# Pipelined attention with score runs of eight heads, a maximum and an exponent over two PSUM banks, and another order of products within a step

## The chip, the cores and the metric

The kernel runs on one core of one Trainium2 chip. The metric is the device time of one execution in microseconds (us); lower is better. The engines are TensorE (PE in the rows; PEld are its weight loads), VectorE (DVE), ScalarE (ACT), GpSimd (POOL) and SyncE (SP), which issues most transfers.

## What is computed

Two decoder layers on x, 32 batches of 128 tokens of width 128, in fp32: self-attention, cross-attention and a mixture of experts, then an attention with shared heads, a masked cross-attention and a second mixture. The change concerns the three attentions with 16 heads of width 8. For one of them the reference has

```python
Q, K, V = proj(q, w_q, b_q), proj(k, w_k, b_k), proj(v, w_v, b_v)   # per head: 128 x 8
scores = jnp.einsum('bhsd,bhtd->bhst', Q, K) / sqrt(8)
attn = jax.nn.softmax(scores, axis=-1)       # the masked one: -1e10 where mask == 0
x = x + (attn @ V, heads joined) @ w_o.T + b_o
```

with a layer norm ahead of each part.

## The kernel before

`head_attention` computes the first two attentions in one pipeline (names with `heads_`, 64 batches, no mask) and, later, the masked one in a second (names with `cross_`, 32 batches). The program is written by hand for each engine, as a function `emit(t)` per engine that says what the engine does in step `t.k`; the waits on semaphores between the engines are written out. One step works on several batches at once, for step k:

- **scores for the maximum** of batch k + 3 (MA = 3), written to `ps_max`, and **scores for the exponent** of batch k, written to `ps_exp`. Q and K are split into three bf16 parts, stacked on 48 rows, so one matrix product gives a head's 128 x 128 scores. The exponent's product has two rows more, with the negated maxima ("shift", split into two bf16 parts). Eight heads lie on rows 0 to 63, eight on rows 64 to 127 (the two halves), and a product for the maximum on one half runs beside one for the exponent on the other (a pair).
- the **maxima** (VectorE, L770) and the **exponents** (ScalarE, L844), which read those banks, in four units of four heads (UNITS = 4). `ps_max` and `ps_exp` have two banks each; unit u uses bank u % 2. So `scores(u)` waits for the maximum and the exponent of unit u - 2, and bank 0 can be filled while bank 1 is read.
- **values** (L992), the products of batch k - 1's exponents with V, two units after `scores(0)` and two after `scores(1)`; then the transposes `turn_spread` (L1041), the division by the sum (L789, L792), the transpose `turn_o` (L1048) and, a step later, the output product (L1054), the residual sum (L784) and the statistics of the next layer norm (L309).
- the **shift**: cast (L798) and remainder (L800) of the negated maxima, transposed on TensorE (L1035, waits for L800), copied by ScalarE (L856) and placed into the QK tiles by two transfers (L606).
- every other step, for a pair of batches (a group) further ahead: normalisation (L306), transposes of x (L1001), projections of Q and K (L1015, L1016) and V (L1026), the split into parts on GpSimd (L683 to L686), their store to DRAM (L690) and their load into the QK tiles (L621, three windows per half).

In the masked pipeline `scores` first writes the mask by products with an identity matrix (L960, L963: 64 x 64 blocks, 512 columns each), four per unit, two for each of the two tiles, and the score products add to that.

`ps_pv` holds the values' products, then the result of `turn_spread`; so `values` of the next batch waits until L792 has read it. `ps_qk` holds the projections of Q and K and, between, the transposed shift.

TensorE's order in a step is: scores(0), values of units 0 and 1, the shift's transpose, scores(1), values of units 2 and 3, output, (even steps) transposes of x, scores(2), turn_spread, (odd) projections of Q and K, scores(3), (even) projection of V, turn_o. VectorE's order is: maxima 0 and 1, residual sum, maximum 2, reciprocal and product, maximum 3, cast and remainder of the shift, statistics, (odd) normalisation and aggregates. SyncE issues the two shift rows first, then the QK loads.

Other parts (the mixtures, the shared-head attention) are untouched. Conversions of expert weights (L244 on ScalarE, L249 on GpSimd) are spread over steps of both pipelines.

## Time and profile before

| | us |
|---|---|
| median of 3 runs | 1090.24 (1085.68 to 1093.18) |
| the profiled execution, first to last instruction | 1087.7 |
| TensorE busy | 973.1 (89%) |
| VectorE busy | 855.0 (79%) |
| ScalarE busy | 692.1 (64%) |
| GpSimd busy | 649.3 (60%) |

A busy TensorE is not TensorE at its peak: matrix products are pipelined and their ends are modelled, and products on different rows of the array overlap. Rows of the timeline give the start, the duration, the engine, the line, the operation, and what it writes and reads, with its size; "x4" says that rows were merged, and the bracket how long the engine was idle before and what ended that. The first maximum starts at 31.0 us, the last of the unmasked pipeline at 351.8; those of the masked one run from 736.9 to 914.2.

### The profile page before, as it was taken

The numbers are of one execution on the slowest core, as the hardware profiler recorded it, in microseconds if no ns is written. First come the engines' busy times: TensorE is split into PE (matmuls) and PEld (weight loads), VectorE is DVE, ScalarE is ACT, GpSimd is POOL, SyncE is SP. The second block draws the span as 40 slices with busy tenths as digits, with TensorE's granted clock in tenths as the row PEclk, the third lists the DMA queues.
The fourth block names the chain that finished last, engine by engine and source line by source line (L and its number), as shares of the span: only waits on it lengthen the run. The fifth ranks groups of instructions, "written<-read, shape, count | busy, mean of one in ns | idle before, by whom it ended". The sixth has DMA issues, their size and how long they took to land.

```text
span 1087.7 us, 33962 instructions
## 1 busy us (share of the span) xinstructions
PE 973.1 (89%) x10494; PEld 694.1 (64%) x10494; DVE 855.0 (79%) x2398; ACT 692.1 (64%) x1801; POOL 649.3 (60%) x1020
## 2 busy tenths in 40 slices
PE   3699999989998888999998889889999999768997
PEld 2466666656665667777776677665656655556885
DVE  6588899888888778888887888776787877657665
ACT  1377777777776743555665887673666666546775
POOL 8757778877676466640675786168667752323443
PEclk9599999999998979999998999998999999989999
DMA  5776567985666201332332111035555640054551
GB/s 147 181 148 132 116 139 163 185 162 134 143 153 171 74 34 50 98 105 77 106 104 55 37 31 38 26 64 133 115 113 129 130 106 18 6 196 167 194 193 29
DMA packets 81460, 119.69 MB, mean 110 GB/s; under 512 B 16720, under 2 KB 62704, under 8 KB 80288
## 3 DMA queue, kind: packets, MB, share of 16 engines
q1 hardware_dynamic: 66704, 85.24, 32.9%
q0 software_dynamic: 9472, 27.27, 8.2%
q10 hardware_dynamic: 5136, 5.31, 2.5%
q8 instruction: 80, 1.31, 0.6%
q14 instruction: 68, 0.56, 0.2%
HBM read 80.75 MB, written 36.18 MB: 107 GB/s over the span
## 4 chain that ended last, share of the span: by engine, by line
PE 61%; DVE 19%; issue 8%; DMA 5%; ACT 3%; POOL 3%; SPq 1%; DVEq 0%; POOLq 0%; ACTq 0%
PE heads_ps_pv L992 4%; PE heads_ps_max L970 4%; DVE heads_neg_max L770 4%; PE cross_ps_max L960 4%; PE experts_ps_gu L2488 4%; PE cross_ps_max L970 3%; PE cross_ps_pv L992 3%; DMA QK<-heads_qk_parts 2%; PE experts_ps_gu L2490 2%; PE experts_ps_gu L2489 2%; PE heads_ps_out L1054 2%; PE experts_ps_y L2509 2%; PE experts_ps_y L2510 2%; PE experts_ps_hT L2496 1%; PE cross_ps_qk L1316 1%
## 5 line engine op out<-in xcount | busy, mean ns | idle before, releaser
L770 DVE TENSOR_REDUCE heads_neg_max<-heads_ps_max 128x4 f32<-128x512 f32 x256 | 169.5, 681 | 36.0 <-PE heads_ps_max L970 34.4
L844 ACT ACTIVATE heads_E<-heads_ps_exp 128x512 f32<-128x512 f32 x256 | 150.1, 603 | 22.1 <-PE heads_ps_pv L992 17.3
L970 PE MATMUL heads_ps_max<-QK 48*128 48x128 bf16 x1024 | 102.9, 226 | 10.2 <-DMA QK<-heads_qk_parts 5.8
L770 DVE TENSOR_REDUCE cross_neg_max<-cross_ps_max 128x4 f32<-128x512 f32 x128 | 86.2, 682 | 29.5 <-PE cross_ps_max L970 28.9
L974 PE MATMUL heads_ps_exp<-QK 50*128 50x128 bf16 x1024 | 103.0, 222 | 0.0
L2182 POOL DMA_INDIRECT experts_gathered<-experts_y_dram,experts_index x64 | 62.0, 969 | 65.4 <-DMA experts_y_dram<-experts_y_sb 44.1
L844 ACT ACTIVATE cross_E<-cross_ps_exp 128x512 f32<-128x512 f32 x128 | 76.5, 599 | 33.1 <-PE cross_ps_exp L974 17.0
L2404 ACT ACTIVATE experts_act_out<-experts_ps_gu 128x256 f32<-128x256 f32 x110 | 42.3, 384 | 83.0 <-PE experts_ps_gu L2490 82.9
L970 PEld LDWEIGHTS heads_ps_max<-QK 48*128 48x128 bf16 x1024 | 58.9, 97 | 52.2 <-issue 21.0
L1613 POOL TENSOR_TENSOR experts_hidden_lo<-experts_hidden,experts_hidden_hi 128x512 fp32r<-128x512 f32 x32 | 41.4, 1293 | 73.9 <-ACT experts_hidden_hi L1837 66.8
L992 PE MATMUL heads_ps_pv<-heads_E,heads_V 128*32 128x128 f32 x2048 | 84.8, 285 | 0.0
L2158 POOL DMA_INDIRECT experts_xs_dram<-QK,experts_index x64 | 61.5, 961 | 33.8 <-DMA experts_xs_dram<-QK,experts_index 22.8
L2509 PE MATMUL experts_ps_y<-experts_down,experts_hT_hi 128*128 (+1 forms) x220 | 67.7, 329 | 6.3 <-DVE experts_hT_lo L2308 4.9
L2303 DVE TENSOR_TENSOR experts_hidden<-experts_act_out,experts_ps_gu 128x256 f32<-128x256 f32 x110 | 46.1, 419 | 25.2 <-ACT experts_act_out L2404 19.2
L1751 DVE TENSOR_TENSOR experts_hidden<-experts_ps_gate,experts_share 128x512 f32<-128x512 f32 x64 | 43.7, 688 | 27.2 <-ACT experts_ps_gate L1831 17.0
L974 PEld LDWEIGHTS heads_ps_exp<-QK 50*128 50x128 bf16 x1024 | 58.3, 96 | 1.5 <-ACT heads_E L844 0.5
L992 PEld LDWEIGHTS heads_ps_pv<-heads_E,heads_V 128*32 128x32 f32 x2048 | 49.7, 111 | 13.6 <-issue 0.4
L2510 PE MATMUL experts_ps_y<-experts_down,experts_hT_lo 128*128 (+1 forms) x220 | 58.0, 285 | 0.0
L1837 ACT CAST experts_hidden_hi<-experts_hidden 128x512 fp32r<-128x512 f32 x72 | 44.2, 615 | 21.2 <-DVE experts_hidden L1751 16.9
L960 PE MATMUL cross_ps_max<-cross_drop_q,identb 64*64 64x512 bf16 x256 | 52.9, 407 | 0.5 <-DVE cross_neg_max L770 0.5
L963 PE MATMUL cross_ps_exp<-cross_drop_k,identb 64*64 64x512 bf16 x256 | 52.9, 407 | 0.0
L1252 ACT ACTIVATE shared_E<-shared_scores,shared_neg_max 128x128 f32<-128x128 f32 x128 | 49.8, 392 | 4.5 <-DVE shared_probs L1201 4.5
(325 smaller groups left out, 3173.3 us busy)
## 6 DMA issues: line engine op xcount, KB each, us to landing
experts_share<-experts_cT_dram SPq DMA_DIRECT2D x7, 2304.0 KB, 8.8
heads_qk_parts<-heads_parts POOLq DMA_DIRECT2D x32, 384.0 KB, 4.7
QK<-heads_qk_parts SPq DMA_DIRECT2D x64, 192.0 KB
QK<-heads_qk_parts SPq DMA_DIRECT2D x64, 128.0 KB
cross_qk_parts<-cross_parts POOLq DMA_DIRECT2D x16, 384.0 KB, 4.2
QK<-cross_qk_parts SPq DMA_DIRECT2D x32, 192.0 KB
experts_xs_dram<-load_stats SPq DMA_DIRECT2D x26, 192.0 KB, 3.0
experts_xs<-experts_xs_dram SPq DMA_DIRECT2D x78, 64.0 KB
```

The costliest lines, as they stand in the source:

```text
L770: nc.vector.tensor_reduce(neg_max[:, half, heads.start:heads.stop], ps_max[:, u % 2, :].rearrange("q (h k) -> q h k", h=HU), AX.X, ALU.max ...
L844: nc.scalar.activation(E[:, half, heads.start:heads.stop, :], ps_exp[:, u % 2, :].rearrange("k (h q) -> k h q", h=HU), ACT.Exp, scale=scal ...
L960: nc.tensor.matmul(ps_max[here, u % 2, :].rearrange("q (h k) -> q h k", h=HU), identb[here, here], drop_q[here].unsqueeze(1).to_broadcast( ...
L963: nc.tensor.matmul(ps_exp[there, u % 2, :].rearrange("k (h q) -> k h q", h=HU), identb[here, here], drop_k[here].unsqueeze(1).to_broadcast ...
L970: last_max = nc.tensor.matmul(ps_max[:, u % 2, i * S:(i + 1) * S], QK[q_of][rows, 0, h, max_of], QK[q_of][rows, 1, h, max_of], start=not m ...
L974: last_exp = nc.tensor.matmul(ps_exp[:, u % 2, i * S:(i + 1) * S], QK[e_of][rows, 1, h, exp_of], QK[e_of][rows, 0, h, exp_of], start=not m ...
L992: last = nc.tensor.matmul(ps_pv[TILE * i:TILE * (i + 1), u // 2 * S:(u // 2 + 1) * S], V[p][:, j, window:window + TILE], E[:, half, h, :], ...
L1252: last = nc.scalar.activation(E[:, s, :], scores[t.k % 2][:, s // 2, s % 2, :], ACT.Exp, bias=neg_max[t.k % 2][:, s:s + 1], accum_out=sums ...
L2158: pool.indirect_dma_start(xs_dram[h], bass.IndirectOffsetOnAxis(index[:, choice, b:b + 1], 0), xn[b // MG][:, b % MG, :], None).then_inc(s ...
L2182: pool.indirect_dma_start(gathered[n % GATHERS][:], None, y_dram[h], bass.IndirectOffsetOnAxis(index[:, choice, b:b + 1], 0)).then_inc(loa ...
L2509: nc.tensor.matmul(out, hT_hi[u % 3][:, these], both, start=c == 0, stop=False, skip_group_check=True)
L2510: last = nc.tensor.matmul(out, hT_lo[u % 3][:, these], both, start=False, stop=c == 1, skip_group_check=True)
```

## The change

Four units become two pairs of units. `scores(v)` now writes eight heads, both banks of `ps_max` and of `ps_exp`, first the four pairs with the maximum on rows 0 to 63, then the four with the halves exchanged; in the masked pipeline the eight mask products of both banks stand ahead of them. One maximum reads both banks of `ps_max` (128 x 1024), one exponent both of `ps_exp`. A run waits until the maximum and the exponent of the run before are done. The values of a pair are eight products as before two units were; those of the first pair now stand in the same step as their exponent (`values(t, 0, 0)`, near the step's end), those of the second pair in the next step. On VectorE the residual sum, the statistics and the normalisation stand behind the first maximum, the reciprocal and the product ahead of the second. On ScalarE the copy L860 of the values stands ahead of the shift's copy L856. SyncE issues the QK loads ahead of the shift rows.

```diff
-UNITS = 4
-HU = H // UNITS
+PAIRS = 2
+HU = H // PAIRS // 2
...
-            def maxima(t, u):
+            def maxima(t, v):
...
-                    dve.wait_ge(max_scored, t.batch(UNITS, MA * UNITS + u + 1))
-                    if u == 0:
+                    dve.wait_ge(max_scored, t.batch(PAIRS, MA * PAIRS + v + 1))
+                    if v == 0:
                         need(dve, shift_ready, t.batch(1, MA))
-                    half, heads = heads_of(u)
-                    nc.vector.tensor_reduce(neg_max[:, half, heads.start:heads.stop], ps_max[:, u % 2, :].rearrange("q (h k) -> q h k", h=HU),
+                    nc.vector.tensor_reduce(neg_max[:, :, heads_of(v)], ps_max[:].rearrange("q a (h k) -> q a h k", h=HU),
                                             AX.X, ALU.max, negate=True).then_inc(max_taken, 1)
...
-            def exp_unit(t, u):
-                act.wait_ge(exp_scored, t.batch(UNITS, u + 1))
-                need(act, pv_done, t.batch(UNITS, -UNITS + u + 1))
-                half, heads = heads_of(u ^ 1)
-                nc.scalar.activation(E[:, half, heads.start:heads.stop, :], ps_exp[:, u % 2, :].rearrange("k (h q) -> k h q", h=HU), ACT.Exp,
+            def exponents(t, v):
+                act.wait_ge(exp_scored, t.batch(PAIRS, v + 1))
+                need(act, pv_done, t.batch(PAIRS, -PAIRS + v + 1))
+                nc.scalar.activation(E[:, :, heads_of(v), :], ps_exp[:].rearrange("k a (h q) -> k a h q", h=HU), ACT.Exp,
                                      scale=scale).then_inc(exp_done, 1)
...
-                    need(pe, max_taken, t.batch(UNITS, MA * UNITS + u - 1))
+                    need(pe, max_taken, t.batch(PAIRS, MA * PAIRS + v))
...
-                    need(pe, exp_done, t.batch(UNITS, u - 1))
...
+                    need(pe, exp_done, t.batch(PAIRS, v))
+                for half in range(HALVES):
+                    for r in range(2):
...
+                for half in range(HALVES):
+                    for i in range(HU):
+                        h = v * HU + i
+                        if with_max:
+                            rows = rows_of(half, ROWS)
+                            last_max = nc.tensor.matmul(ps_max[:, half, i * S:(i + 1) * S], QK[q_of][rows, 0, h, max_of], QK[q_of][rows, 1, h, max_of],
+                                                        start=not masked, stop=True, skip_group_check=masked)
+                        if with_exp:
+                            rows = rows_of(1 - half, ROWS + SHIFT)
+                            last_exp = nc.tensor.matmul(ps_exp[:, 1 - half, i * S:(i + 1) * S], QK[e_of][rows, 1, h, exp_of], QK[e_of][rows, 0, h, exp_of],
+                                                        start=not masked, stop=True, skip_group_check=masked)
...
+                scores(t, 0)
+                if prev:
+                    values(t, 1, 1)
+                if nxt:
+                    turn_shift(t)
+                if t.has(2, NB_ALL + 1):
+                    output(t)
+                if front:
+                    transpose_x(t)
+                scores(t, 1)
+                if prev:
+                    turn_spread(t)
+                if not even and t.has(1 - 2 * FA, 2 * NG_ALL - 1 - 2 * FA):
+                    project_qk(t)
                 if even and t.has(-2 * VA, 2 * NG_ALL - 2 - 2 * VA):
                     project_v(t)
+                if now:
+                    values(t, 0, 0)
                 if prev:
                     turn_o(t)
```

TensorE, second half of an odd step of the unmasked pipeline, before; the rows begin in the last score pair of the third unit (`heads_ps_max` and `heads_ps_exp` are the scores, `heads_ps_pv` the values and their transposes, `heads_ps_qk` the projections):

```order
L970 MATMUL heads_ps_max<-QK 128x128
L974 MATMUL heads_ps_exp<-QK 128x128
L1041 MATMUL heads_ps_pv<-ident,heads_oT_spread 128x128 x2
L1015 MATMUL heads_ps_qk<-heads_xnT,heads_wq 128x256
L1016 MATMUL heads_ps_qk<-heads_xnT,heads_wk 128x256
L83 REGISTER_ALU
L970 MATMUL heads_ps_max<-QK 128x128
L974 MATMUL heads_ps_exp<-QK 128x128
```

The same place in the changed program, from the last pair of its second score run:

```order
L961 MATMUL heads_ps_max<-QK 128x128
L965 MATMUL heads_ps_exp<-QK 128x128
L1032 MATMUL heads_ps_pv<-ident,heads_oT_spread 128x128 x2
L1006 MATMUL heads_ps_qk<-heads_xnT,heads_wq 128x256
L1007 MATMUL heads_ps_qk<-heads_xnT,heads_wk 128x256
L983 MATMUL heads_ps_pv<-heads_E,heads_V 32x128 x8
L1039 MATMUL heads_ps_out<-ident,heads_o_tok 128x128
L83 REGISTER_ALU
```

The score run that stood behind the projections is gone from there (it is part of the second run), and eight products of values stand in its place.

VectorE, an even step of the unmasked pipeline before, from the residual sum on (`heads_neg_max` is the maximum, `heads_o_tok` the divided values, `norm_stats` the statistics):

```order
L784 TENSOR_TENSOR x_sb<-heads_ps_out,x_sb 128x128
L766 REGISTER_ALU
L770 TENSOR_REDUCE heads_neg_max<-heads_ps_max 128x4
L788 REGISTER_ALU
L789 RECIPROCAL heads_recip<-heads_ps_pv 128x16
L792 TENSOR_TENSOR heads_o_tok<-heads_ps_pv,heads_recip 128x128
L766 REGISTER_ALU
L770 TENSOR_REDUCE heads_neg_max<-heads_ps_max 128x4
L798 CAST heads_shift<-heads_neg_max 128x2x8
L799 REGISTER_ALU
L800 TENSOR_TENSOR heads_shift<-heads_neg_max,heads_shift 128x2x8
L309 BN_STATS norm_stats<-x_sb 128x6
```

The same step in the changed program:

```order
L781 TENSOR_TENSOR x_sb<-heads_ps_out,x_sb 128x128
L309 BN_STATS norm_stats<-x_sb 128x6
L789 REGISTER_ALU
L790 RECIPROCAL heads_recip<-heads_ps_pv 128x16
L793 TENSOR_TENSOR heads_o_tok<-heads_ps_pv,heads_recip 128x128
L765 REGISTER_ALU
L768 TENSOR_REDUCE heads_neg_max<-heads_ps_max 128x2x4
L799 CAST heads_shift<-heads_neg_max 128x2x8
L800 REGISTER_ALU
L801 TENSOR_TENSOR heads_shift<-heads_neg_max,heads_shift 128x2x8
```

The third maximum is gone from ahead of the reciprocal, the fourth has become the second, wider one, and the statistics have moved ahead of the reciprocal.

SyncE, two steps of the unmasked pipeline before (`heads_qk_parts` are the split Q and K in DRAM, `heads_shiftT` the shift rows):

```order
L606 DMA QK<-heads_shiftT 2x8x128 x2
L613 ISA
L83 REGISTER_ALU
L621 DMA QK<-heads_qk_parts 24x2x2048
L621 DMA QK<-heads_qk_parts 16x2x2048
L621 DMA QK<-heads_qk_parts 8x2x2048
L602 REGISTER_ALU
L606 DMA QK<-heads_shiftT 2x8x128 x2
```

The changed program:

```order
L611 DMA QK<-heads_qk_parts 24x2x2048
L611 DMA QK<-heads_qk_parts 16x2x2048
L611 DMA QK<-heads_qk_parts 8x2x2048
L617 ISA
L621 DMA QK<-heads_shiftT 2x8x128 x2
```

Within a step the three loads have moved ahead of the two shift rows.

## Rows read from the trace of the kernel before

**Rows 1.** Windows: stretch, length, busy us per engine, clock, DMA share, GB/s.
```profile
200.00:280.00 80.00, 72.87 (x1188) 48.16 (x1186) 69.16 (x187) 59.68 (x145) 59.73 (x106) 1.00 0.77 158
770.00:910.00 140.00, 139.07 (x2248) 83.30 (x2240) 111.96 (x292) 93.21 (x224) 85.96 (x157) 1.00 0.50 112
```

**Rows 2.** Line L895: duration ns min/median/max, first and last start.
```profile
L895 ACT ACTIVATE heads_oT<-heads_ps_out,heads_bv x64: 367/370/380, 59.0 to 374.6; 128x128 f32<-128x128 f32 x64
L895 ACT ACTIVATE cross_oT<-cross_ps_out,cross_bv x32: 361/373/379, 763.8 to 938.8; 128x128 f32<-128x128 f32 x32
```

**Rows 3.** Waits, 80 to 330 us: total us, times, longest us.
```profile
PEld heads_ps_qk L1035 <- DVE heads_shift L800: 15.5, 27, 1.3
...
PE heads_ps_qk L1035 <- DVE heads_shift L800: 8.7, 23, 1.1
...
PE heads_ps_max L970 <- DMA QK<-heads_qk_parts: 2.8, 3, 1.1
PEld heads_ps_max L970 <- DMA QK<-heads_qk_parts: 2.3, 2, 1.2
```

**Rows 4.** Timeline, 180 to 188 us, two steps without a mask.
```profile
180.47 0.24 DVE L789 RECIPROCAL heads_recip<-heads_ps_pv 128x16 f32<-128x16 f32 x1
180.75 0.29 DVE L792 TENSOR_TENSOR heads_o_tok<-heads_ps_pv,heads_recip 128x128 f32<-128x128 f32 x1
...
180.95 0.68 DVE L770 TENSOR_REDUCE heads_neg_max<-heads_ps_max 128x4 f32<-128x512 f32 x1
...
183.15 0.64 PE L992 MATMUL heads_ps_pv<-heads_E,heads_V 128*32 128x128 f32 x16
...
183.73 0.49 PE L1054 MATMUL heads_ps_out<-heads_wo,heads_oT 128*128 128x128 f32 x2
...
184.13 1.09 ACT L844 ACTIVATE heads_E<-heads_ps_exp 128x512 f32<-128x512 f32 x2
...
184.15 0.23 PE L970 MATMUL heads_ps_max<-QK 48*128 48x128 bf16 x1
...
184.33 0.22 PE L970 MATMUL heads_ps_max<-QK 48*128 48x128 bf16 x1
...
184.48 0.44 PE L1041 MATMUL heads_ps_pv<-ident,heads_oT_spread 128*128 128x128 f32 x2
...
184.75 0.60 PE L1015 MATMUL heads_ps_qk<-heads_xnT,heads_wq 128*128 128x256 f32 x2
...
185.71 0.23 PE L970 MATMUL heads_ps_max<-QK 48*128 48x128 bf16 x1
...
186.14 0.69 DVE L770 TENSOR_REDUCE heads_neg_max<-heads_ps_max 128x4 f32<-128x512 f32 x1 [0.38 <-PE heads_ps_max L970]
...
186.87 0.17 DVE L798 CAST heads_shift<-heads_neg_max 128x16 bf16<-128x16 f32 x1
...
186.94 0.67 POOL L684 TENSOR_TENSOR heads_rest<-heads_qk_full,heads_parts 128x256 f32<-128x256 f32 x1
...
187.08 0.56 DVE L800 TENSOR_TENSOR heads_shift<-heads_neg_max,heads_shift 128x16 bf16<-128x16 f32 x1
...
187.69 0.23 PE L1035 MATMUL heads_ps_qk<-identb,heads_shift 128*32 128x128 bf16 x1 [0.42 <-DVE heads_shift L800]
```

**Rows 5.** VectorE's groups by form: busy us, mean ns of one, idle before.
```profile
L770 DVE TENSOR_REDUCE heads_neg_max<-heads_ps_max 128x4 f32<-128x512 f32 x256 | 169.5, 681 | 36.0 <-PE heads_ps_max L970 34.4 <-issue 0.7
...
L800 DVE TENSOR_TENSOR heads_shift<-heads_neg_max,heads_shift 128x16 bf16<-128x16 f32 x64 | 21.9, 342 | 2.2
...
L306 DVE TENSOR_SCALAR heads_xn<-x_sb,norm_mean,norm_rstd 128x128 f32<-128x128 f32 x32 | 13.0, 497 | 0.3 <-POOL norm_rstd L301 0.3
...
L2272 DVE TENSOR_REDUCE experts_tile_of<-experts_ended 128x39 f32<-128x312 f32 x2 | 1.0, 478 | 0.1
```

**Rows 6.** Timeline, masked pipeline: the four mask products, then the first score product.
```profile
849.16 0.40 PE L960 MATMUL cross_ps_max<-cross_drop_q,identb 64*64 64x512 bf16 x1
...
849.50 0.23 PE L970 MATMUL cross_ps_max<-QK 48*128 48x128 bf16 x1
```

More of the change, by code:

```diff
@@ L957, in scores @@
-                for r in range(2):
-                    here, there = slice(r * BASE, (r + 1) * BASE), slice((1 - r) * BASE, (2 - r) * BASE)
-                    if masked and with_max:
-                        nc.tensor.matmul(ps_max[here, u % 2, :].rearrange("q (h k) -> q h k", h=HU), identb[here, here],
-                                         drop_q[here].unsqueeze(1).to_broadcast([BASE, HU, S]), start=True, stop=False, skip_group_check=True)
-                    if masked and with_exp:
-                        nc.tensor.matmul(ps_exp[there, u % 2, :].rearrange("k (h q) -> k h q", h=HU), identb[here, here],
-                                         drop_k[here].unsqueeze(1).to_broadcast([BASE, HU, S]), start=True, stop=False, skip_group_check=True)
```

137 lines of the change are left out of this document (55 added, 82 removed).

## The prediction

> **What bounds the kernel now.** I read the busy times by stretch first. The pipelined attention takes up two stretches: layers 1 and 2 (64 batches, no mask) and the masked layer (32 batches). In the unmasked stretch TensorE is busy 72.87 of 80 us and VectorE 69.16; in the masked one TensorE 139.07 of 140 and VectorE 111.96; in both stretches TensorE has its full clock [rows 1]. The copies L895 come once a step, so their first and last starts give the step: (374.6 - 59.0)/63 = 5.01 us unmasked, (938.8 - 763.8)/31 = 5.65 us masked [rows 2]. So a tenth of a microsecond a step is 6 us on layers 1 and 2 and 3 us on the masked layer.
>
> Next the waits of the unmasked stretch. TensorE's longest is for the shift (L1035 for L800, 15.5 us in the weight loads and 8.7 in the products); 5.1 us go to waits for QK loads [rows 3]. Neither engine is the bound alone: they hand work back and forth, and the step is a chain of both. The timeline shows the links [rows 4]. The masked layer is different: there TensorE has no gaps, so only a shorter TensorE list or a new stall can move it.
>
> **What the change removes.** Four maxima of 512 columns become two of 1024. One of 512 takes 0.681 us, a reduction of 312 columns 0.478 [rows 5]: 1.02 ns a column, so 1024 columns take 0.68 + 0.52 = 1.20 us. Per step 2.40 in place of 2.72 us by durations. Exponents: two of 512 columns that follow each other take 1.09 us (184.13 [rows 4]); I take 1.05 for one of 1024 (bounds 0.55 and 1.09, one or two of the old). TensorE's matrix products stay the same in number; two switches between a score run and other work go.
>
> **What it adds.** Each score run now writes both banks of ps_max and ps_exp, so it must wait until the previous maximum and exponent have emptied both. Before, a run filled one bank while the other was read. I lay one unmasked step out by links, from the first score product:
> - to the start of the maximum: 0.43 us with four pairs (185.71 to 186.14); a further pair costs 0.06 (184.15 to 184.33 for three), so 0.67 with eight
> - the maximum, 1.20; its release of TensorE 0.05, as L800's end at 187.64 to L1035 at 187.69
> - the second score run's issue, 0.33 with four pairs (184.15 to 184.48), 0.57 with eight; then the two transposes L1041, 0.44 and 0.03 to VectorE
> - reciprocal 0.28 and product 0.20 up to the next start (180.47, 180.75, 180.95), because they stand ahead of the second maximum on VectorE
> - the second maximum 1.20 and the release 0.05.
>
> All of these are in [rows 4]. Sum: 0.67 + 1.20 + 0.05 + 0.57 + 0.47 + 0.48 + 1.20 + 0.05 = 4.69 us.
>
> TensorE's other work lies under the two maxima. First gap (0.10 + 1.20 + 0.05 = 1.35 after the issue): second half of values 0.58 (183.15 to 183.73), the shift's transpose 0.2, output 0.42 (183.73 to 184.15), in even steps two transposes of x more. Second gap (0.47 + 0.48 + 1.20 + 0.05 = 2.2): L1041's issue 0.27, a projection of up to 0.96 (184.75 to 185.71), first half of values 0.58, transpose of o 0.3. The sums are 1.2 to 1.5 and up to 2.1, so both gaps are nearly full, and the exponent ends ahead of the maximum. If that cover fails, each 0.1 over is 6 us on 64 steps.
>
> The shift's split moves out of TensorE's way: L800 now has the score run and half of values to hide under, so TensorE's waits for it should go. What is late next is VectorE itself. Between the two maxima across a step's end it has 0.05 + 0.67 = 0.72 us for the cast (0.04 + 0.21) and L800 (0.18 free; it took 0.56 where a GpSimd instruction ran at its start, and ended at 187.64, with GpSimd's L684 at 187.61 [rows 4]), in odd steps also 0.2 for the two aggregates. Free, this fits. Blocked for 0.56 to 0.73 it overhangs by 0.1 to 0.45. L800's mean of 342 ns [rows 5] between 175 and about 640 says that 36% are blocked: 0.36 x 0.28 = 0.10 a step; if all are blocked, 0.28. The Trainium skill's page "SBUF — State Buffer" (Who interferes with whom) says that a VectorE instruction with two SBUF inputs contends with GpSimd instructions that read SBUF; the trace agrees, 0.56 us against 0.18. By the page every call that meets one would block.
>
> In odd steps the normalisation (two of about 0.5 us at most [rows 5]) now stands between the first maximum and the reciprocal, behind the residual sum and the statistics: together about 1.25 us against a cover of 0.05 + 0.57 + 0.47 = 1.09. Overhang 0.15 every other step, 0.07 a step; nothing where the three pipeline well.
>
> Step: 4.69 + 0.10 + 0.07 = 4.86, against 5.01 a gain of 0.15 (bounds: a gain of 0.32 with no overhang, a loss of 0.03 with every call blocked). Of the 64 steps some 56 run full at full clock: **-8 us** (-18 to +2).
>
> QK loads are issued ahead of the shift rows. Until now SyncE waits for L856 and issues two shift rows ahead of them; the loads leave earlier by that, and the 5.1 us of waits [rows 3] should go. They are part of the 5.01, so I add nothing. Behind the load's own wait (scores of the previous step, done as the step begins) now stand the shift rows, needed two steps later: no price.
>
> **The masked layer.** Eight mask products stand ahead of eight pairs, behind the wait for both banks. Four cost 0.34 (849.16 to 849.50 [rows 6]). The second four go into the same quadrants with 512 columns each, as many as four pairs' columns in a row, 0.24: I take 0.58 (bounds 0.34, were they free, and 0.68, twice). The step is then 1.25 + 1.20 + 0.05 + 1.15 + 0.47 + 0.48 + 1.20 + 0.05 = 5.85 us; at the bounds 5.37 and 6.05. TensorE's own list, 5.65 now, shrinks by 4 x 0.33 - 2 x 0.57 on pairs and 4 x 0.34 - 2 x 0.58 on masks to 5.27, so the chain sets the step. Of 32 steps some 28 are full: +0.20 x 28 = **+6 us** (-8 to +11). Here the Trainium skill speaks against the change: "Perfetto Trace Analysis" (Optimizing Scalar/DVE Operations) says that grouping operations helps where their engine is saturated, and that where it is not but causes bubbles on others, breaking them up lets work end sooner. VectorE is busy 80% and TensorE 99% here [rows 1]; by that rule the masked layer gets slower, as by my sum.
>
> **Start of the layers.** Six steps (three at each start) have maxima alone, whose runs and maxima now alternate strictly; 0.2 us each by the 0.05 + 0.10 of each handover, **+1 us**.
>
> **Sum.** -8 + 6 + 1 = -1 against the profiled 1087.7 us; the median of the three runs is 2.5 us above that execution. I predict 1089 us: no change. A change below 1% (11 us) can't be told from none by this measurement.
>
> **Rivals.**
> 1. Faster: VectorE is the real bound of layers 1 and 2, L800 finds GpSimd idle at its new place and the normalisation pipelines, so the step is the bare chain, 4.69: -18 us; with the mask products overlapping near 0.34 the masked layer adds -2 to -8. For it: the waits for L800 are the largest [rows 3]. Against it: GpSimd's order follows the same projections, so it should meet L800 as often. About 1069 us.
> 2. Slower: one pair of banks, filled and read by turns. With every L800 blocked the unmasked step gets 5.04 (+2 us), the masked one 6.05 (+11 us), and if the even steps' 1.5 us of TensorE work overruns the first gap of 1.35, +0.15 on half of 56 steps and on 14 masked ones gives +6: about 1109 us. For it: in the masked layer nothing but TensorE is full [rows 1]. Against it: the gap holds in odd steps. It decides where the chain passes 5.01 unmasked or 5.65 masked; the second is passed already in my sum.
> 3. ScalarE late: in the 25 or so steps with weight conversions the exponent starts behind them and holds the next score run, which before had a second bank; 0.3 us each, +7 us: 1096 us, still within the 1%. The exponent ends 0.1 us ahead of the maximum, so it decides once ScalarE is over 0.1 us late.
>
> **How the numbers follow.** No change (my sum, with rival 3 inside it): 0.56. Rival 1: 0.25. Rival 2: 0.19. The range 1069 to 1107 leaves out about a tenth on either side: the far ends of rivals 1 and 2. The likeliest case alone is 1080 to 1098.
>
> **What would show it.** In the profile of the changed kernel the maximum should take 1.20 us and the exponent 1.05; L1035's waits for the shift should be nearly gone, and score runs should wait for the maximum in their place, 0.1 to 0.3 us twice a step; no waits for QK loads; unmasked steps of 4.9 and masked ones of 5.85 us; TensorE in the masked stretch clearly below its 99%. Wrong would be: masked steps of 5.65 or less (the mask products overlap more than I think), unmasked ones over 5.05, or score runs that wait for ScalarE.

## The result and the profile after

The changed kernel takes 1131.5 us (median of four runs, 1120.1 to 1143.2), the kernel before 1091.7 beside it: a ratio of 1.034, interval [1.027, 1.041]. It is slower by 3.4%; the prediction was no change, and the time lies above its range. The profiled execution spans 1118.0 us against 1087.7, so 30.3 us are to be found there. It is the fastest of the four; the other three took 8 to 23 us more at lower mean clocks (0.932 to 0.951 against 0.966), and no profile shows where.

The busy times by stretch, as in [rows 1]: start and end, length, busy us of TensorE, its weight loads, VectorE, ScalarE, GpSimd, then granted clock, DMA share, GB/s.

```profile
200.00:280.00 80.00, 66.04 (x997) 46.15 (x998) 64.51 (x131) 49.15 (x99) 52.64 (x92) 0.87 0.60 136
780.00:920.00 140.00, 125.24 (x2120) 77.88 (x2122) 106.19 (x230) 83.39 (x170) 90.92 (x166) 1.00 0.51 117
```

Every engine does less in the unmasked stretch, and TensorE's clock there is 0.87 where it was 1.00. In the masked stretch TensorE has fallen from 99% to 89% busy at full clock.

The copies that mark the steps, as in [rows 2] (duration ns min/median/max, first and last start; the 1st to the 24th, the 24th to the 37th, the 37th to the 58th, all, and those of the masked layer):

```profile
L885 ACT ACTIVATE heads_oT<-heads_ps_out,heads_bv x24: 367/367/368, 59.4 to 175.5; 128x128 f32<-128x128 f32 x24
L885 ACT ACTIVATE heads_oT<-heads_ps_out,heads_bv x14: 367/367/368, 175.5 to 261.8; 128x128 f32<-128x128 f32 x14
L885 ACT ACTIVATE heads_oT<-heads_ps_out,heads_bv x22: 367/367/368, 261.8 to 367.8; 128x128 f32<-128x128 f32 x22
L885 ACT ACTIVATE heads_oT<-heads_ps_out,heads_bv x64: 367/367/368, 59.4 to 397.9; 128x128 f32<-128x128 f32 x64
L885 ACT ACTIVATE cross_oT<-cross_ps_out,cross_bv x32: 367/367/368, 784.4 to 968.6; 128x128 f32<-128x128 f32 x32
```

From the starts of the same copies (L895 in the kernel before), in us:

| stretch | before | after | difference |
|---|---|---|---|
| A: copies 1 to 24, 23 steps, 16 of them in a loop | 112.5 | 116.1 | +3.6 |
| B: copies 24 to 37, 13 steps written out, with expert weights | 67.2 | 86.3 | +19.1 |
| C: copies 37 to 58, 21 steps, 16 in a loop | 105.1 | 106.0 | +0.9 |
| D: copies 58 to 64, the last steps | 30.8 | 30.1 | -0.7 |
| M: the masked layer's 32 copies | 175.0 | 184.2 | +9.2 |
| all else | 597.1 | 595.3 | -1.8 |

(The expectations below call A "copies 0 to 24", B "copies 24 to 36" and C "36 to 57".) Most of the loss is in thirteen steps. Six of them take 7.0 to 9.1 us, from the first score product of one step to that of the next. One, in the timeline (L689 is GpSimd's issue of the store of split Q and K, L703 its addition of the output bias):

```profile
175.44 0.91 POOL L689 DMA_DIRECT2D heads_qk_parts<-heads_parts  x1 [0.29 <-POOL heads_parts L685]
175.60 0.73 DVE L799 CAST heads_shift<-heads_neg_max 128x16 bf16<-128x16 f32 x1
176.36 2.29 DVE L801 TENSOR_TENSOR heads_shift<-heads_neg_max,heads_shift 128x16 bf16<-128x16 f32 x1
176.38 0.74 POOL L703 TENSOR_TENSOR x_sb<-x_sb,heads_bo 128x256 f32<-128x256 f32 x1
177.06 1.54 POOL L249 TENSOR_TENSOR experts_gate_up_lo<-experts_whole,experts_gate_up_hi 128x640 fp32r<-128x640 f32 x1
178.55 0.20 POOL L296 TENSOR_TENSOR norm_var_eps<-norm_moments,norm_eps 128x2 f32<-128x2 f32 x1
178.70 0.23 PE L1026 MATMUL heads_ps_qk<-identb,heads_shift 128*32 128x128 bf16 x1 [1.84 <-DVE heads_shift L801]
178.75 1.23 DVE L768 TENSOR_REDUCE heads_neg_max<-heads_ps_max 128x8 f32<-128x1024 f32 x1
...
180.03 0.28 PE L961 MATMUL heads_ps_max<-QK 48*128 48x128 bf16 x1 [0.38 <-DVE heads_neg_max L768]
```

The cast (L799) is held until the issue of GpSimd's store is nearly over. So the remainder (L801, the L800 of before) starts just behind that issue and 0.02 us ahead of the bias addition L703. It ends 0.05 us behind the weight remainder L249, which follows L703 without a gap: 2.29 us where it takes 0.18 free. (The small L296, which follows without a gap too, does not prolong it.) The maximum (L768) of the next score run waits behind it on VectorE, and both the shift's transpose and the next run wait for those; TensorE stands idle for 1.84 us. Then its clock falls (windows):

```profile
175.00:179.00 4.00, 1.94 (x43) 1.23 (x35) 3.83 (x4) 2.20 (x5) 3.68 (x7) 0.98 0.88 158
179.00:186.00 7.00, 6.62 (x69) 4.46 (x73) 4.34 (x13) 2.61 (x6) 2.26 (x5) 0.52 0.51 122
```

0.52 of full speed is near the lower of its two levels, 1.2 of 2.4 GHz. In the kernel before, the remainder met the same GpSimd work but earlier. In its longest calls it began inside the issue of the store and was over 0.04 us before that issue ended, after 0.74 us at most; the bias addition (L704 there) came behind it:

```profile
181.74 0.91 POOL L690 DMA_DIRECT2D heads_qk_parts<-heads_parts  x1 [0.29 <-POOL heads_parts L686]
181.88 0.73 DVE L800 TENSOR_TENSOR heads_shift<-heads_neg_max,heads_shift 128x16 bf16<-128x16 f32 x1
182.68 0.74 POOL L704 TENSOR_TENSOR x_sb<-x_sb,heads_bo 128x256 f32<-128x256 f32 x1
```

The waits from 80 to 330 us, as in [rows 3]:

```profile
PEld heads_ps_max L961 <- DVE heads_neg_max L768: 22.1, 47, 0.8
PE heads_ps_max L961 <- DVE heads_neg_max L768: 20.0, 59, 0.9
...
PEld heads_ps_qk L1026 <- DVE heads_shift L801: 9.8, 6, 2.1
PE heads_ps_qk L1026 <- DVE heads_shift L801: 8.2, 6, 1.8
```

The waits for the shift are down from 27 and 23 times to 6 each, the held ones; score runs wait for the maximum instead, 0.3 to 0.5 us each on average where 0.1 to 0.3 was foreseen; there is none for QK loads.

### The profile page after: what moved, and what is told of

Same layout as the page of the kernel before. It is cut to its first block, busy times and chain, and to the rows that moved or that the text cites. A ratio compares the mean times of both kernels' runs of the same rounds, so it can differ in the third digit from the quotient of the medians.

```text
span 1118.0 us, 33012 instructions
## 1 busy us (share of the span) xinstructions
PE 943.0 (84%) x10494; PEld 689.8 (62%) x10494; DVE 854.9 (76%) x2206; ACT 671.7 (60%) x1609; POOL 649.0 (58%) x1020
## 4 chain that ended last, share of the span: by engine, by line
PE 51%; DVE 29%; issue 9%; ACT 4%; POOL 3%; DMA 2%; DVEq 1%; SPq 0%; POOLq 0%; ACTq 0%
DVE heads_neg_max L768 9%; DVE cross_neg_max L768 4%; PE experts_ps_gu L2480 3%; PE heads_ps_max L961 3%; PE cross_ps_max L951 3%; PE experts_ps_gu L2482 2%; PE experts_ps_gu L2481 2%; PE heads_ps_pv L983 2%; PE heads_ps_exp L965 2%; PE cross_ps_max L961 2%; PE heads_ps_pv L1032 2%; PE cross_ps_pv L983 2%; PE experts_ps_y L2501 2%; PE experts_ps_y L2502 1%; PE experts_ps_hT L2488 1%
## 5 line engine op out<-in xcount | busy, mean ns | idle before, releaser
L768 DVE TENSOR_REDUCE heads_neg_max<-heads_ps_max 128x8 f32<-128x1024 f32 x128 | 156.1, 1219 | 39.3 <-PE heads_ps_max L961 36.5
L838 ACT ACTIVATE heads_E<-heads_ps_exp 128x1024 f32<-128x1024 f32 x128 | 131.0, 1023 | 70.9 <-PE heads_ps_exp L965 70.6
L961 PE MATMUL heads_ps_max<-QK 48*128 48x128 bf16 x1024 | 85.1, 230 | 40.7 <-DVE heads_neg_max L768 29.1
L961 PEld LDWEIGHTS heads_ps_max<-QK 48*128 48x128 bf16 x1024 | 62.3, 100 | 67.7 <-DVE heads_neg_max L768 32.9
L838 ACT ACTIVATE cross_E<-cross_ps_exp 128x1024 f32<-128x1024 f32 x64 | 65.5, 1024 | 61.0 <-PE cross_ps_exp L965 61.0
L768 DVE TENSOR_REDUCE cross_neg_max<-cross_ps_max 128x8 f32<-128x1024 f32 x64 | 78.0, 1219 | 17.5 <-PE cross_ps_max L961 17.2
L965 PE MATMUL heads_ps_exp<-QK 50*128 50x128 bf16 x1024 | 82.2, 226 | 0.4
L682 POOL TENSOR_SCALAR heads_parts<-heads_qk_full 128x256 bf16<-128x256 f32 x64 | 25.9, 405 | 61.6 <-ACT heads_qk_full L870 54.6
L951 PE MATMUL cross_ps_max<-cross_drop_q,identb 64*64 64x512 bf16 x256 | 39.9, 385 | 18.2 <-DVE cross_neg_max L768 11.9
```

The costliest lines, as they stand in the source:

```text
L768: nc.vector.tensor_reduce(neg_max[:, :, heads_of(v)], ps_max[:].rearrange("q a (h k) -> q a h k", h=HU), AX.X, ALU.max, negate=True).then_ ...
L838: nc.scalar.activation(E[:, :, heads_of(v), :], ps_exp[:].rearrange("k a (h q) -> k a h q", h=HU), ACT.Exp, scale=scale).then_inc(exp_done, 1)
L951: nc.tensor.matmul(ps_max[here, half, :].rearrange("q (h k) -> q h k", h=HU), identb[here, here], drop_q[here].unsqueeze(1).to_broadcast([ ...
L961: last_max = nc.tensor.matmul(ps_max[:, half, i * S:(i + 1) * S], QK[q_of][rows, 0, h, max_of], QK[q_of][rows, 1, h, max_of], start=not ma ...
L965: last_exp = nc.tensor.matmul(ps_exp[:, 1 - half, i * S:(i + 1) * S], QK[e_of][rows, 1, h, exp_of], QK[e_of][rows, 0, h, exp_of], start=no ...
```

## The experiments

Ratios are against the kernel before, with their 95% interval, which reaches about one point to either side; so two runs whose ratios differ by a point are hardly told apart by them. The letters are the stretches above, in the profiled execution.

**Weight remainders a step later** (seven of eight; the eighth could not go into the loop that follows):

```diff
-                    if 1 <= t.k - WORK <= EACH * SPLIT_PIECES and (t.k - WORK - 1) % EACH == 0:
-                        prepare.take_lo(nc, pool, (t.k - WORK - 1) // EACH, prep_hi, prep_lo)
+                    lo_steps = [min(WORK + EACH * (i + 1), WORK + EACH * SPLIT_PIECES - EACH + 1) for i in range(SPLIT_PIECES)]
+                    if t.k in lo_steps:
+                        prepare.take_lo(nc, pool, lo_steps.index(t.k), prep_hi, prep_lo)
```

> Theory A: the six steps of 7.0 to 9.1 us in layers 1 and 2 come from VectorE's shift remainder (L801), which starts just as GpSimd begins the bias addition (L703) and is held until the remainder of an expert weight (L249) behind it has ended too, 2.0 to 2.3 us. Here seven of the eight weight remainders are issued one step later, behind the norm's last work, so that nothing follows the bias addition directly. A expects no remainder L801 above 0.8 us, TensorE's granted clock at 1.00 throughout 80 to 330 us, and 16 to 20 us less than the changed kernel (six steps at 5.1 to 5.4 instead of 8.5). Rival B: the pair form with one set of banks is slow by itself there, and the half clock comes from its gaps; then the long steps stay wherever GpSimd's work stands, and the time is within 5 us of the changed kernel.

B takes 69.9 us, 16.4 less. The remainder is held long once, by the eighth piece (2.29 us), and TensorE's clock falls twice: behind that hold, and behind a wait of 1.4 us for a late shift row. So the two expectations of no long hold and of a full clock throughout failed by the piece that was left and by a wait that theory A didn't have. The steps whose piece was moved have no long hold, which bears theory A out against rival B. The ratio is 1.018 [1.008, 1.029], 1.6 points (17 us) below the changed kernel's. In the profiled execution stretch D takes 43.2 us against 30.1, at a clock of 0.58 from 350 to 400 us (1.00 in the changed kernel's): that stays open, see below.

**Which pipeline**: a kernel with both bodies, chosen by the mask; the second run has `mask is not None`.

```diff
+    body = head_attention_units if mask is None else head_attention_pairs
```

> Layers 1 and 2 as before (units of four heads, two maxima in flight, the old order on all engines), the masked layer in the changed form. If the two pipelines add up, the loss of layers 1 and 2 (22.9 us by the copies in the profiled runs) goes and that of the masked layer (9.2 us) stays: 8 to 11 us over the kernel before. If the slowdown were a matter of what layers 1 and 2 leave behind for later stages, more would go.

> The other half: layers 1 and 2 in the changed form, the masked layer as before. By adding up, 20 to 27 us over the kernel before, with the six long steps in the trace; masked steps of 5.65 us in place of 5.90.

Ratios 1.018 [1.009, 1.027] and 1.021 [1.011, 1.031]. The first keeps the masked layer's 184.6 us (774.0 to 958.6); the second has it back at 175.1 and keeps B at 84.6, with five long holds in place of six (four of the remainder and one, of 2.41 us, of the cast). Both halves are slower, as expected. The first lost some 19 us by the ratio (give or take 10), more than its masked part of 9.6; in its profiled execution 7 of that lie in D (37.8 us). It also shows one thing that the kernel before did not. With the old form and two banks the remainder met the row once in layers 1 and 2 (L801, L705 and L250 here):

```profile
236.15 2.27 DVE L801 TENSOR_TENSOR heads_shift<-heads_neg_max,heads_shift 128x16 bf16<-128x16 f32 x1
238.48 0.29 PE L1036 MATMUL heads_ps_qk<-identb,heads_shift 128*32 128x128 bf16 x1 [2.24 <-DVE heads_shift L801]
```

TensorE stood idle for 2.24 us, the clock was 0.50 from 238.4 to 245 us, and the step took 10.0 us. So two banks don't protect from a long hold; the kernel before escaped it because the two never met in its trace.

**The gap filled**, so that the hold stays and TensorE doesn't stand idle:

```diff
+                if not masked and t.reg is None and t.k - WORK in range(3, EACH * SPLIT_PIECES, EACH):
+                    pe.wait_ge(oT_ready, t.batch(1, -1))
+                    need(pe, x_done, t.batch(1, -2))
+                    for i in range(24):
+                        nc.tensor.matmul(ps_out[:, 1, :], identb[:], identb[:], start=True, stop=True)
                 if nxt:
                     turn_shift(t)
```

> The changed kernel with 24 more matrix products of 128 columns in each of the seven steps in which the shift remainder can be held (TensorE, between the second half of values and the turn of the shift, written where the output product writes over them; they change no result). They fill the gap of 1.84 us in which TensorE stood idle. Theory A1: part of a long step is TensorE's half clock behind that gap (0.41 us in the second score run, 0.3 in the turn, 1.2 at the step's end, 0.3 in the next step); then L801 is still held for 2.0 to 2.3 us, the granted clock stays at 1.00, long steps shrink from 8.3 to 9.1 to some 7.0, and 7 to 10 us go. Rival: the length comes from GpSimd's late split and the queue behind L801 alone; then nothing goes, and up to 2 us come on top.

B takes 78.9 us, 7.4 less, which mixes fewer holds, full clock and the fills' own time; so the steps are read singly, from the first product of a second score run to that of the next. Three are held with the gap filled and take 7.22, 7.23 and 7.10 us. A fourth, past the last fill, is held as long and takes 9.15. The two kinds side by side, first with the fill, then without:

```profile
179.93 2.29 DVE L801 TENSOR_TENSOR heads_shift<-heads_neg_max,heads_shift 128x16 bf16<-128x16 f32 x1
...
249.35 2.28 DVE L801 TENSOR_TENSOR heads_shift<-heads_neg_max,heads_shift 128x16 bf16<-128x16 f32 x1
```
```profile
179.50:186.50 7.00, 5.76 (x97) 4.19 (x93) 6.70 (x11) 4.01 (x8) 3.99 (x7) 1.00 0.69 138
248.50:257.80 9.30, 6.93 (x74) 4.48 (x75) 7.67 (x15) 3.71 (x7) 4.48 (x7) 0.66 0.56 141
```

So a hold of 2.3 us costs some 2 us by itself and, through the clock, 1.9 more. The changed kernel's own sixth hold agrees without any fill: 2.24 us long, it left TensorE idle for 1.21 us, the clock stayed at 1.00 and the step took 7.02 us. The whole kernel gained little (1.031 [1.022, 1.040]), since in four steps that were not held the fill cost 1.2 us each.

**All weight remainders ahead of the split**, without and with SyncE's old order:

```diff
                 if not even and t.has(1 - 2 * FA, 2 * NG_ALL - 1 - 2 * FA):
+                    if t.reg is None and prepare.splits and 1 <= t.k - WORK <= EACH * SPLIT_PIECES:
+                        prepare.take_lo(nc, pool, (t.k - WORK - 1) // EACH, prep_hi, prep_lo)
                     split(t)
...
-                    if 1 <= t.k - WORK <= EACH * SPLIT_PIECES and (t.k - WORK - 1) % EACH == 0:
-                        prepare.take_lo(nc, pool, (t.k - WORK - 1) // EACH, prep_hi, prep_lo)
+                    if EACH == 1 and even and 1 <= t.k - WORK <= SPLIT_PIECES:
+                        prepare.take_lo(nc, pool, t.k - WORK - 1, prep_hi, prep_lo)
```

> The changed kernel with all eight weight remainders (L249) issued ahead of GpSimd's split of the same step and not behind its bias addition (the run with the weights a step later had moved seven, and the eighth still held VectorE for 2.29 us). By the theory that the back-to-back pair of GpSimd instructions holds the shift remainder, none is now held above 0.8 us, and copies 24 to 36 of layers 1 and 2 take 60 to 66 us (86.3 in the changed kernel, 69.9 with seven moved). What may remain is waits for the shift rows' transfer, which the new order of SyncE puts behind the QK loads (3.9 us in four waits with seven moved). Rival: another pair of GpSimd's instructions takes its place and holds as long; then it stays near 70.

> The same, and on SyncE the shift rows are issued ahead of the QK loads again, as in the kernel before. If the new SyncE order makes the score runs wait for the shift rows, those waits (3.9 us with seven remainders moved) go and copies 24 to 36 get 2 to 4 us shorter than in the run without it; waits for QK loads come in their place if the loads were late by the old order (5.1 us in the kernel before). If SyncE's order is free, as the prediction had it, both take the same within 1 us.

(B has thirteen steps; where an expectation says twelve, it miscounts.) With the new SyncE order B takes 65.9 us and no remainder in it exceeds 0.63 us; ratio 1.012 [1.005, 1.019]. With the old order B takes 70.9; ratio 1.014 [1.006, 1.022], not told apart by the times. The waits for transfers from 80 to 330 us, the old order first, then the new:

```profile
PEld heads_ps_max L963 <- DMA QK<-heads_qk_parts: 5.0, 5, 2.6
PE heads_ps_max L963 <- DMA QK<-heads_qk_parts: 4.3, 5, 2.4
```
```profile
PE heads_ps_max L963 <- DMA QK<-heads_shiftT: 1.6, 1, 1.6
```

So the new SyncE order does what it seems to: QK loads are in time, at the price of a late shift row now and then. The one here left TensorE idle for 1.63 us, and its step took 7.2 us between copies.

**The same edit in the kernel before.**

> The kernel before with the weight remainders ahead of GpSimd's split. In that kernel the shift remainder slipped into the gap before the bias addition, so the long hold did not arise, yet copies 24 to 36 took 67.2 us for 12 steps, 5.6 each against 5.0 elsewhere. If that, too, is VectorE held by GpSimd, it gets 2 to 6 us faster; if it is ScalarE's and the transfers' load, nothing moves. It is also a candidate for the best version.

Ratio 0.998 [0.992, 1.005], B 66.5 us: nothing. The pair on GpSimd cost the kernel before nothing. (5.6 a step in the expectation is 5.17 with thirteen steps.)

**Loops written out** (the lead of the masked pipeline's too):

```diff
-            steps(sp, emit, FIRST, LOOPS, LAST)
+            steps(sp, emit, FIRST, [], LAST)
```

and the same on the other engines.

> The changed kernel with the loops of both pipelines written out (32 of the 64 steps, and 8 of the 32 masked ones, run in loops of eight steps). In loops, every other score run starts 0.23 us after the maximum's end where 0.06 to 0.10 is the rule, with a register operation and a separate wait between them on TensorE's queue; the normalisation's link is longer there too (0.61 to 0.98 against 0.48). Theory: computing a wait's value costs time where a run and a maximum alternate strictly; written out, copies 0 to 24 and 36 to 57 then shrink from 116.1 and 106.0 us by 2 to 4 each, and steps of 4.8 appear. Rival: those links are VectorE held by GpSimd and have nothing to do with loops; then nothing goes. The six long steps stay in both cases.

Ratio 1.011 [1.003, 1.019]. A takes 111.1 us (5.0 less), C 101.6 (4.4 less), and steps of 4.72 and 4.86 alternate; B still has three holds of 2.0 to 2.3 us and takes 73.7. In the changed kernel's loops some score runs begin late, though not every other one as the expectation had it: between 75 and 156 us 7 of 32 begin 0.22 to 0.29 us behind the maximum's end, the rest 0.05 to 0.13; written out, all begin within 0.10. One of either kind:

```profile
93.15 1.22 DVE L768 TENSOR_REDUCE heads_neg_max<-heads_ps_max 128x8 f32<-128x1024 f32 x1
...
94.42 0.23 PE L961 MATMUL heads_ps_max<-QK 48*128 48x128 bf16 x1 [0.18 <-DVE heads_neg_max L768]
...
98.27 1.21 DVE L768 TENSOR_REDUCE heads_neg_max<-heads_ps_max 128x8 f32<-128x1024 f32 x1
...
99.72 0.21 PE L961 MATMUL heads_ps_max<-QK 48*128 48x128 bf16 x1 [0.37 <-DVE heads_neg_max L768]
```

From the maximum's end 0.05 us at 94.42, 0.24 at 99.72. The control is the kernel before with its loops written out:

> The control for it: the kernel before with its loops written out. If the cost of computing a wait's value falls on the path only where a run and a maximum alternate strictly, this gains nothing: steps stay at 5.0 us, within 3 us of the kernel before. If written-out loops help any form, copies 0 to 24 and 36 to 57 get 4 to 5 us shorter each, as in the changed kernel.

Ratio 0.997 [0.992, 1.002]; A 114.6 us, C 105.0: nothing gained. The control isn't clean: with the loops written out 52 of its 64 remainders are held for 0.56 to 0.75 us, where 24 are in the kernel before, and that may hide a gain. (With 28 more short holds A to C together are 0.9 us longer than in the kernel before.) In the changed kernel a part of what the loops cost is VectorE's: between 74 and 156 us nine casts took 0.54 to 0.71 us, where one (0.73) did with the loops written out. By their lengths the seven late starts make up about 1.2 of the 5.0 us that A gained and the held casts 3 to 4; no run tells the two apart.

**A better version**: pairs in layers 1 and 2 with both repairs, units in the masked layer.

> A version that should beat both kernels: layers 1 and 2 in the changed form, with the weight remainders ahead of GpSimd's split and all loops written out; the masked layer as before. From the runs so far: copies 0 to 24 take 111.1 us and 36 to 57 take 101.6 (the run with loops written out; 112.5 and 105.1 in the kernel before), copies 24 to 36 take 58 to 66 (67.2), the masked layer as before: 6 to 14 us under the kernel before, ratio 0.987 to 0.995. If the gains of the two edits don't add up, it lands within 1% of the kernel before on either side.

Ratio 0.991 [0.987, 0.995] from five rounds, 1088.7 us against 1096.8 beside it: faster than the changed kernel by far, and than the kernel before by little. Over all runs beside it the means differ by 0.7%, and the profiled executions span 1087.4 and 1087.7 us; so that gain is likely and not certain. A takes 110.7 us, B 64.5, C 104.1 (its last step already at the lower clock), the masked layer 174.6. D takes 38.4 against 30.8 and eats part of the gain.

**The whole change with both repairs.**

> The whole change, masked layer too, with both repairs (weight remainders ahead of the split, loops written out). By adding up the stages of the runs so far: the masked layer 7 to 9 us over the kernel before, layers 1 and 2 8 to 14 under it: within 6 us of the kernel before, which is what the prediction had for the change itself. If the prediction's chain were wrong and not only its two missing costs, it stays 10 us or more over the kernel before.

Ratio 1.006 [1.000, 1.011]: near the kernel before, as the prediction had it for the change itself. So with the two costs mended nothing large is left but D, 44.5 us in its profiled execution.

**What in the row holds VectorE.** First the weight remainders as fills, which read nothing:

```diff
-        nc.gpsimd.tensor_tensor(lo, whole, hi.bitcast(F32), ALU.subtract).then_inc(lo_made, 1)
+        nc.gpsimd.memset(lo.bitcast(F32), 0.0).then_inc(lo_made, 1)
```

> The changed kernel with the weight remainders on GpSimd (L249, two inputs from SBUF) replaced by fills with zero of the same tiles, at the same places; this leaves the lower parts of the expert weights out of the result. It tells apart what in the GpSimd row behind the bias addition holds VectorE. By the Trainium skill's page SBUF — State Buffer (Who interferes with whom), an instruction with two SBUF inputs is held only by GpSimd work that reads SBUF: then the shift remainder is held for the bias addition alone, 0.55 to 0.8 us, and the long steps shrink to 5.4 or less. Rival: any GpSimd instruction in the row holds it, then L801 takes 0.74 us plus the fill's duration.

1112.4 us in one run, B 72.1. The remainder was never held long, but it didn't meet a row either: with the first hold gone, the later ones no longer came to the row's start. The cast met one of the eight rows, and the fill did hold it: from inside the store's issue, through the bias addition, to 0.03 us behind the fill's end.

```profile
241.15 1.87 DVE L799 CAST heads_shift<-heads_neg_max 128x16 bf16<-128x16 f32 x1
...
242.35 0.64 POOL L249 MEMSET experts_gate_up_lo<- 128x640 f32 x1
```

(Its other long steps are waits of up to 2.3 us for late shift rows.) For the remainder this doesn't tell, so the row was tied to VectorE's pair, with the real remainder and with the fill:

```diff
+                    if EACH == 2 and t.reg is None and 1 <= t.k - WORK <= EACH * SPLIT_PIECES:
+                        pool.wait_ge(max_taken, t.batch(PAIRS, (MA + 2) * PAIRS))
                     xg = x_sb[:, bass.ds(t.group(G, (FA - of * NG) * G), G), :]
```

> The changed kernel with one more wait: in the eight steps with a weight remainder GpSimd begins its bias addition (L703) only when the second maximum of the next step has ended, so the row of L703 and L249 starts together with VectorE's cast and shift remainder every time, where the changed kernel meets it in six of eight. If the row holds VectorE to its end, cast and remainder together end 0.03 to 0.06 us after L249 does, 2.0 to 2.4 us after the row's start, in all eight. If VectorE gets in between L703 and L249, they are over after 0.8 to 1.1 us.

> The same with L249 replaced by a fill with zero of the same tile (0.54 or 0.64 us, no input; the lower parts of the expert weights are left out of the result). The run with fills alone did not tell, since VectorE's two instructions no longer met the row. By the Trainium skill's page SBUF — State Buffer (Who interferes with whom), two SBUF inputs are held only by GpSimd work that reads SBUF: then the remainder ends with L703 or 0.2 us behind it, 0.8 to 1.1 us after the row's start. Rival: any GpSimd instruction in the row holds it: 0.05 us behind the fill's end, 1.3 to 1.5 us after the row's start.

The wait made them meet in three rows of eight with the real remainder and in four with the fill, not in all. One of each, cast L801, remainder L803, bias addition L705 here:

```profile
197.07 0.91 POOL L689 DMA_DIRECT2D heads_qk_parts<-heads_parts  x1 [0.29 <-POOL heads_parts L685]
197.41 2.86 DVE L801 CAST heads_shift<-heads_neg_max 128x16 bf16<-128x16 f32 x1
198.01 0.75 POOL L705 TENSOR_TENSOR x_sb<-x_sb,heads_bo 128x256 f32<-128x256 f32 x1
198.70 1.54 POOL L249 TENSOR_TENSOR experts_gate_up_lo<-experts_whole,experts_gate_up_hi 128x640 fp32r<-128x640 f32 x1
```
```profile
208.02 0.80 DVE L803 TENSOR_TENSOR heads_shift<-heads_neg_max,heads_shift 128x16 bf16<-128x16 f32 x1
208.04 0.74 POOL L705 TENSOR_TENSOR x_sb<-x_sb,heads_bo 128x256 f32<-128x256 f32 x1
208.70 0.54 POOL L249 MEMSET experts_gate_up_lo<- 128x512 f32 x1
```

In all three rows with the real weight remainder it is the cast that is held, to 0.03 to 0.04 us behind L249 (2.51 to 2.86 us), and VectorE's remainder follows free. In all four with the fill it is VectorE's remainder, and it is free 0.04 to 0.05 us behind the bias addition. So the two runs don't compare the same instruction. The remainder's comparison is with the changed kernel, where all six that met the row were held to the end of the real L249: the fill doesn't hold the remainder, with its two inputs from SBUF. It does hold the cast, in the one row above. Whether the fill lets the remainder go because it reads nothing, or because it is short (0.54 to 0.65 us against 1.27 to 1.54), is not told apart: in the masked layer real weight remainders of 0.46 to 0.73 us, which read SBUF, let it go as well. In layers 1 and 2 a hold thus lasts through the bias addition and the weight remainder behind it; that it always lasts through work without a gap is not shown (L296 above, and the masked layer below).

## Why the prediction failed

The chain that it laid out, link by link, against the step from 89.68 to 94.42 us, which nothing held:

```profile
89.68 0.21 PE L961 MATMUL heads_ps_max<-QK 48*128 48x128 bf16 x1 [0.37 <-DVE heads_neg_max L768]
...
90.34 1.23 DVE L768 TENSOR_REDUCE heads_neg_max<-heads_ps_max 128x8 f32<-128x1024 f32 x1 [0.17 <-PE heads_ps_max L961]
...
91.62 0.23 PE L961 MATMUL heads_ps_max<-QK 48*128 48x128 bf16 x1
...
92.17 0.44 PE L1032 MATMUL heads_ps_pv<-ident,heads_oT_spread 128*128 128x128 f32 x2
92.65 0.26 DVE L790 RECIPROCAL heads_recip<-heads_ps_pv 128x16 f32<-128x16 f32 x1 [0.33 <-PE heads_ps_pv L1032]
```

| link | predicted | measured |
|---|---|---|
| score run to maximum | 0.67 | 0.66 |
| maximum (twice) | 1.20 | 1.23, 1.22 |
| its release of TensorE (twice) | 0.05 | 0.05 |
| second run's issue | 0.57 | 0.55 |
| transposes to VectorE | 0.47 | 0.48 |
| reciprocal and product | 0.48 | 0.50 |
| sum | 4.69 | 4.74 |

- **The chain: right.** The exponent, 1.05, measures 1.02. Where loops and holds are away, steps alternate between 4.72 and 4.86, a mean of 4.79 against a bare 4.69 and the 4.86 with both overhangs; the normalisation's 0.15 every other step is there (0.14).
- **"Blocked for 0.56 to 0.73 it overhangs by 0.1 to 0.45": the step that failed, by its size.** The longest blocked remainder that the old trace showed was taken for the longest there can be. Six were held for 2.0 to 2.3 us. The share was too high, 14 of 64 held and not 36%, but the cast, priced at 0.04 + 0.21 whatever it met, was held too, for up to 0.82 us. The old trace had the sign of both: one cast there was held for 1.46 us, to 0.04 behind the end of a long weight conversion.

```profile
327.33 1.53 POOL L249 TENSOR_TENSOR experts_down<-experts_whole,experts_down 128x640 fp32r<-128x640 f32 x1
327.44 1.46 DVE L798 CAST heads_shift<-heads_neg_max 128x16 bf16<-128x16 f32 x1
```

- **Full clock throughout: failed.** Five of the six long holds left a gap (1.1 to 1.8 us) behind which the clock fell to about half. Against the filled steps with a hold of the same length (7.22 and 7.10), those five, 8.34 to 9.07, are 1.2 to 1.9 longer, 7.5 us together of B's 19.1; the holds themselves are most of the rest. (It is an estimate: the filled steps hold the fills' time too, and the step behind each is 0.3 longer where the clock was low.)
- **"Its release of TensorE 0.05": right, but not in loops.** Writing the loops out gave back 9.4 us in A and C together, 0.29 for each of 32 steps. That holds both the late starts and most of the cast's holds there, and is why A and C lost 4.5 us instead of gaining the predicted 0.15 a step.
- **QK loads: right**, no waits. What that is worth in the changed kernel was not run; with the weights moved the new order is 5.0 us shorter in B, not told apart by the times. "No price" for the later shift rows holds in the changed kernel; once steps are shorter it is a wait of 1.6 us, and 1.4 at most with the weights a step later.
- **The masked layer: right in mechanism, small in size.** Eight mask products cost 0.56 (0.58 predicted), the step is 5.90 (5.85), and three remainders of 0.80 us make three steps of 6.30. That gives +9.2 where +6 stood. The rows (the first mask product, the first score product behind the eight, the maximum):

```profile
807.80 0.37 PE L951 MATMUL cross_ps_max<-cross_drop_q,identb 64*64 64x512 bf16 x1 [0.15 <-issue]
...
808.36 0.23 PE L961 MATMUL cross_ps_max<-QK 48*128 48x128 bf16 x1
...
809.02 1.23 DVE L768 TENSOR_REDUCE cross_neg_max<-cross_ps_max 128x8 f32<-128x1024 f32 x1 [0.25 <-PE cross_ps_max L961]
```

- **Rivals.** The second had the direction and the alternating banks, but its price (every call held, gaps overrun) was for another mechanism. The first was the bare chain; the runs that repair the change come near it (4.79 against 4.69), but with the normalisation's overhang and a slower masked layer. The third, a late ScalarE, is not seen: the profile puts nine weight loads between 80 and 330 us down to an exponent (5.0 us), but ahead of every score run there the exponent had ended before the maximum.

What stays open: why D takes 30 to 31 us in nine of the sixteen profiled executions and 36 to 45 in seven, with granted clocks of 0.50 to 0.71 from 350 to 400 us in these seven. It happened in both forms (37.8 in the kernel before with its weights moved), and mostly where layers 1 and 2 had got shorter, so it may give back gains; no run tells that. Nor is it shown why the masked layer's remainder was free behind the bias addition (0.80 us, three times) although a weight remainder followed there as well, without a gap; it was of 128 or 256 columns there and of 512 or 640 in layers 1 and 2.

## What to carry to other kernels

An instruction that can be held by another engine is not bounded by the longest hold that one trace shows of it: look for the longest row of instructions without a gap on the other engine, and ask whether the change lets the two meet at its start. Where work strictly alternates between two engines, a short hold lies on the path (the three masked steps of 6.30 us); with a second buffer 28 more of them came with 0.9 us in all, but a long hold cost as much there too (the step of 10.0 us). Before taking such a change, move long work of the other engine to where the held one is not due.

## What the runs showed of the hardware

- The Trainium skill, "SBUF — State Buffer" (Who interferes with whom), says that the instruction which issues second is blocked until the first is over. Here it was blocked through two instructions in a row, 2.0 to 2.9 us, and the remainder even where it showed its start 0.02 us ahead of the row's; in the masked layer through the first alone (0.80 us). The page's restriction, for two SBUF inputs, to GpSimd work that reads SBUF is not contradicted: behind the bias addition the fill did not hold the remainder in four of four rows, but nor did the masked layer's weight remainders, which read SBUF and are as short as the fill.
- A cast with a single SBUF input was held as well (2.86 us), by the fill too (1.87 us, one row), and by GpSimd's DMA issue for 0.73 us, as the remainder was in the kernel before; batch statistics from SBUF never were:

```profile
L309 DVE BATCH_NORM_STATS2 norm_stats<-x_sb x49: 293/294/297, 61.6 to 326.2; 128x6 f32 x31, 128x6 f32<-128x128 f32 x18
```

- TensorE's clock fell to about half behind five single idle times of 1.1 to 1.8 us in the changed kernel, not behind a sixth of 1.2, and stayed at 1.00 when plain products filled them.
- Holds came in a series: six of the seven weight rows from 176 to 256 us met VectorE's pair at their start. With fills in their place it met one of eight; that a hold sets the place of the next one is argued, not shown.
